# A decoder block's first phases: v kept unflipped, the long filter's matrices loaded row by row into the first phase and kept on the chip

## What is computed

```python
h = layernorm(x)                                      # 16 x 256 x 256
q, k, v = (silu(causal_dwconv(h @ W, w_conv)) for W, w_conv in ...)   # 4 taps per channel
beta, res = sigmoid(h @ Wb), sigmoid(h @ Wres + bres)
q, k = l2norm(q), l2norm(k)
inv = inverse of (I + strictly lower part of (beta k) k^T), in chunks of 32 tokens
long_fir[t, c]  = sum over j < 64 of fir_long[c, 63 - j] * v[t - j, c]    # one filter per channel
short_fir[t, c] = the same with 5 taps
```

## Time and profile before

| what | us |
|---|---|
| time, median of 3 runs | 1337.79 |
| lowest and highest of them | 1335.50, 1341.93 |
| profiled execution, from its first to its last instruction | 1347.3 |
| phase A in it | 0 to 245.2 |
| phase B in it | 245.4 to 324.2 |
| the rest in it | 324.5 to 1347.3 |
| DVE busy in phases A and B | 200.7 of 245 and 77.3 of 80 |

### The profile page before, as it was taken

The page is one execution under the profiler, slowest core; times in us unless marked ns, Lnnn a source line. Parts: engine busy times, 40 slices in busy tenths (PEclk is TensorE's granted clock), DMA queues, the critical chain, the costliest instruction groups (busy, mean ns, idle before and its releaser), DMA issues. The chain is left out here.

```text
span 1347.3 us, 28551 instructions
## 1 busy us (share of the span) xinstructions
PE 1128.1 (84%) x9177; PEld 829.4 (62%) x9251; DVE 957.8 (71%) x2132; ACT 900.2 (67%) x1743; POOL 658.3 (49%) x2200
## 2 busy tenths in 40 slices
PE   5989898783777879999999999999999887885756
PEld 4767676683566656766766776676676654443225
DVE  4999998698345666767777866876776666633985
ACT  4989998221343567778778878867877765453867
POOL 4777775663135455365465556446546544111007
PEclk9999999555567889899999989989989999997989
DMA  2444433894313333323434434334332342203106
GB/s 77 149 153 160 167 141 149 185 226 119 120 56 103 95 102 107 112 91 111 128 109 122 124 102 135 103 106 126 107 111 84 83 144 64 75 33 123 58 1 218
DMA packets 141779, 154.17 MB, mean 114 GB/s; under 512 B 48040, under 2 KB 106560, under 8 KB 141632
## 3 DMA queue, kind: packets, MB, share of 16 engines
q1 hardware_dynamic: 141632, 152.35, 37.5%
HBM read 93.32 MB, written 58.72 MB: 113 GB/s over the span
## 5 line engine op out<-in xcount | busy, mean ns | idle before, releaser
L2119 DVE TENSOR_REDUCE x_maxima<-x_psA 128x2 f32<-128x512 f32 x248 | 170.8, 689 | 116.3 <-PE x_psA L1447 114.4
L1703 ACT ACTIVATE x_PT<-x_psB 128x512 f32<-128x512 f32 x240 | 143.0, 596 | 53.8 <-PE x_psB L1471 49.5
L1710 ACT ACTIVATE x_psA<-x_mask_q 128x512 f32<-128x512 bf16 x239 | 142.5, 596 | 48.9 <-DVE x_maxima L2119 45.8
L297 DVE SCALAR_TENSOR_TENSOR a_conv<-a_ps_proj,taps,a_conv 128x253 f32<-128x253 f32 (+2 forms) x288 | 115.0, 470 | 10.6 <-ACT a_conv L364 10.6
L1447 PE MATMUL x_psA<-x_Ks,x_Qs 96*128 96x256 bf16 x496 | 99.1, 282 | 17.7 <-ACT x_psA L1710 17.2
L533 PE MATMUL a_ps_proj<-a_hT,wqkv 128*128 128x256 f32 x384 | 95.9, 401 | 6.4 <-DVE a_conv L297 3.8
L1471 PE MATMUL x_psB<-x_Qs,x_Ks 98*128 98x256 bf16 x480 | 93.2, 275 | 8.0 <-issue 6.4
L533 PEld LDWEIGHTS a_ps_proj<-a_hT,wqkv 128*128 128x128 f32 x384 | 73.1, 198 | 19.5 <-issue 6.1
L1863 POOL TENSOR_SCALAR x_parts_q<-x_rest 128x512 bf16<-128x512 f32 x16 | 23.9, 1496 | 115.1 <-DVE x_rest L2095 115.1
L1468 PE MATMUL x_psB<-x_mask_k,x_ident_bf 128*128 128x512 bf16 x170 | 66.2, 390 | 13.3 <-ACT x_PT L1703 10.8
L1485 PE MATMUL x_psO<-x_PT,x_V 128*32 128x256 f32 x1024 | 70.9, 396 | 1.1 <-ACT x_PT L1703 1.0
(11 more groups left out here) (390 smaller groups left out, 3344.6 us busy)
## 6 DMA issues: line engine op xcount, KB each, us to landing
scratch_keypack<-a_keypack SPq DMA_DIRECT2D x16, 768.0 KB, 3.3
c_keypack<-scratch_keypack SPq DMA_DIRECT2D x16, 768.0 KB, 4.7
x_Ks<-scratch_k_parts SPq DMA_DIRECT2D x192, 64.0 KB, 2.2
b_matrix<-in_long_padded SPq DMA_DIRECT2D x16, 512.0 KB, 6.9
scratch_k_parts<-x_parts_k SPq DMA_DIRECT2D x32, 192.0 KB, 2.4
scratch_q_parts<-x_parts_q SPq DMA_DIRECT2D x32, 192.0 KB, 2.3
x_Qs<-scratch_q_parts SPq DMA_DIRECT2D x32, 192.0 KB, 2.9
a_x_in<-in_x SPq DMA_DIRECT2D x16, 256.0 KB, 2.7
```

The lines of the kernel that those rows point to most:

```text
L297: nc.vector.scalar_tensor_tensor(acc, ps_proj[PROJ_BANK[p]][:, c, 0:L - j], taps[:, p, c, TAPS - 1 - j:TAPS - j], acc, ALU.mult, ALU.add). ...
L1703: nc.scalar.activation(PT[:, k % (2 * GROUP)], bank_B(b, k)[0], ACT.Exp, scale=XD ** -0.5).then_inc(pexp_ready, 1)
L1710: nc.scalar.activation(psA[:].rearrange("p t q -> p (t q)"), mask_q[:, k % 2].rearrange("p s k -> p (s k)"), ACT.Copy).then_inc(mask_writt ...
L2119: nc.vector.tensor_reduce(maxima[:, t, 2 * pair:2 * pair + 2], bank_A(b, k)[0], AX.X, ALU.max).then_inc(maxed, 1)
```

## The change

Phase A no longer flips v. ACT's `vtok` copies v straight into `v_windows[:, 1]`, and the store of v reads it there. Two DMAs of a new operation `win` copy v, shifted by 64 tokens, within SBUF into `v_windows[:, 0]`. `v_tok`, both flips, their matrices, their three copies and their waits are gone.

With v the right way up the band matrix has to be reversed instead, so each partition starts one element earlier than the one before it. The matrices of all 256 channels are kept in a new buffer `matrix` [128, 256, 64], and phase A loads it partition by partition: 8 rows in each of the turns 0 to 15, by four operations `rows0` to `rows3` of SP, two loads each. SP waits for all of them at the end of phase A.

Phase B has no matrix loads. One matmul per channel takes both windows (64 columns), and the two halves of the channels go to the two halves of the output's partitions. There are 16 groups of 8 channel pairs, with 8 buffers in PSUM. The result is stored by eight DMAs in two stages. The early loads for phase C are all issued at the start of phase B. To make room, the buffers of the inversion lie in `X32` and `shared` now, so that each of the transposes waits for the one before.

```diff
-A_ORDER = [(0, "ld_x"), (4, "silu_v"), (1, "rstd"), (5, "kpk"), (3, "proj_q"), (3, "tap_q"), (3, "conv_k"), (4, "tail"),
-           (4, "norms"), (4, "norm"), (2, "turn_h"), (2, "hTc"), (5, "flipA"), (4, "ktok"), (5, "st_p"), (4, "st_k"),
-           (3, "conv_q"), (5, "diag"), (4, "stap"), (5, "dk"), (5, "fA"), (3, "tanh"), (3, "silu_q"), (2, "proj_k"),
+A_ORDER = [(0, "ld_x"), (0, "rows0"), (4, "silu_v"), (1, "rstd"), (5, "kpk"), (3, "proj_q"), (3, "tap_q"), (3, "conv_k"), (4, "tail"),
+           (4, "norms"), (4, "norm"), (2, "turn_h"), (2, "hTc"), (4, "ktok"), (5, "st_p"), (4, "st_k"), (0, "rows1"),
+           (3, "conv_q"), (5, "diag"), (4, "stap"), (5, "dk"), (3, "tanh"), (3, "silu_q"), (2, "proj_k"),
            (4, "short1"), (3, "silu_k"), (3, "proj_v"), (3, "tap_v"), (4, "tok2"), (4, "vtok"), (2, "tap_k"), (2, "gate"),
-           (0, "stat"), (4, "short2"), (3, "st_hT"), (3, "gsc"), (4, "st_v"), (3, "tok0"), (3, "sq0"), (4, "short_t"),
-           (4, "stok"), (1, "xn"), (4, "flipB"), (2, "gbias"), (4, "ks"), (4, "ksT"), (3, "tok1"), (4, "fB"), (3, "sq1"),
+           (0, "stat"), (4, "short2"), (0, "rows2"), (3, "st_hT"), (3, "gsc"), (4, "st_v"), (4, "win"), (0, "rows3"), (3, "tok0"), (3, "sq0"), (4, "short_t"),
+           (4, "stok"), (1, "xn"), (2, "gbias"), (4, "ks"), (4, "ksT"), (3, "tok1"), (3, "sq1"),
            (4, "st_s"), (3, "conv_v")]
...
+W_LOADS = 16 * 9
+FIR_COLS = P + HB
+ROWS_PER_TURN = P // B
+P_PER_SEM = 16
...
-        v_tok = sb("a_v_tok", [P, TT, D])
...
-        short_tok = sb("a_short_tok", [P, TT, D])
+        short_tok = keep["shared"][:, 0, 2]
...
-        squares = sb("a_squares", [P, 2, TT, D])
+        squares = keep["shared"][:, 0, 0:2]
...
                 elif op == "st_v":
                     sp.wait_ge(v_tok_ready, b + 1)
-                    sp.dma_start(dram["v_tok"][b], v_tok[:]).then_inc(v_stored, 16)
+                    sp.dma_start(dram["v_tok"][b], keep["v_windows"][:, 1, :, b]).then_inc(v_stored, 16)
+                elif op[:4] == "rows":
+                    for i in range(ROWS_PER_TURN // 4):
+                        r = ROWS_PER_TURN * b + ROWS_PER_TURN // 4 * int(op[4]) + i
+                        taps_of = bass.AP(dram["long_padded"].tensor, P - 1 - r, [[0, 1], [FIR_COLS, D], [1, HB]])
+                        sp.dma_start(keep["matrix"][r:r + 1], taps_of).then_inc(taps_placed[r // P_PER_SEM], 16)
+                elif op == "win":
+                    sp.wait_ge(v_tok_ready, b + 1)
+                    sp.dma_start(keep["v_windows"][HB:P, 0, :, b], keep["v_windows"][0:HB, 1, :, b]).then_inc(window_set, 16)
+                    sp.dma_start(keep["v_windows"][0:HB, 0, 1, b], keep["v_windows"][HB:P, 1, 0, b]).then_inc(window_set, 16)
...
-            sp.dma_start(flip[:], dram["flip"]).then_inc(w_loaded, 16)
-            sp.dma_start(half_flip[:], dram["half_flip"]).then_inc(w_loaded, 16)
...
                 elif op == "vtok":
                     act.wait_ge(turned[2], b + 1)
-
-                    if b >= 1:
-                        act.wait_ge(v_stored, 16 * b)
-                        act.wait_ge(v_flipped, b)
-                        act.wait_ge(half_flipped, b)
-                    nc.scalar.activation(v_tok[:], ps_tok[2][:], ACT.Copy).then_inc(v_tok_ready, 1)
-                elif op == "fA":
-                    act.wait_ge(v_flipped, b + 1)
-                    nc.scalar.activation(keep["v_windows"][:, 1, :, b], ps_tok[2][:], ACT.Copy).then_inc(flip_kept, 1)
-                elif op == "fB":
-                    act.wait_ge(half_flipped, b + 1)
-                    act.wait_ge(window_zero, 1)
-                    nc.scalar.activation(keep["v_windows"][0:HB, 0, :, b], ps_tok[2][0:HB], ACT.Copy)
-                    nc.scalar.activation(keep["v_windows"][HB:P, 0, 1, b], ps_tok[2][HB:P, 1], ACT.Copy).then_inc(half_kept, 1)
+                    nc.scalar.activation(keep["v_windows"][:, 1, :, b], ps_tok[2][:], ACT.Copy).then_inc(v_tok_ready, 1)
...
                     else:
-                        after(b, (flip_kept, -1, 1), (half_kept, -1, 1), (v_tok_ready, -1, 1))
...
-                elif op == "flipA":
-                    pe.wait_ge(v_tok_ready, b + 1)
-                    after(b, (half_kept, 0, 1), (v_tok_ready, 0, 1), (flip_kept, -1, 1))
-                    nc.tensor.matmul(ps_tok[2][:].rearrange("p t c -> p (t c)"), flip[:], v_tok[:].rearrange("p t c -> p (t c)"),
-                                     start=True, stop=True).then_inc(v_flipped, 1)
-                elif op == "flipB":
-                    pe.wait_ge(v_tok_ready, b + 1)
-                    after(b, (v_tok_ready, 0, 1), (flip_kept, -1, 1), (half_kept, -1, 1))
-                    nc.tensor.matmul(ps_tok[2][0:HB].rearrange("p t c -> p (t c)"), half_flip[:, 0:HB],
-                                     v_tok[:].rearrange("p t c -> p (t c)"), start=True, stop=True)
-                    nc.tensor.matmul(ps_tok[2][HB:P, 1], half_flip[:, HB:P], v_tok[:, 0], start=True, stop=True).then_inc(half_flipped, 1)
...
-CG = 16
-GROUPS = D // CG
-DEPTH = 4
+CG = 8
+GROUPS = P // CG
+DEPTH = 8
 EARLY_AT = 4
-FIR_COLS = P + HB
 
 
 def phase_b(nc, sems, dram, keep, used, early):
...
-        matrix = [sb(f"matrix{i}", [P, CG, HB]) for i in range(DEPTH)]
-        M = sb("M", [P, NQ, CH, CH])
-        product = sb("product", [P, NQ, (CH // 2) * (CH // 2)])
-        lower = sb("lower", [P, CH, CH])
-        psum = [ctx.enter_context(nc.psum_tensor(f"b_ps{i}", [P, CG, TT, B], FP32)) for i in range(DEPTH)]
-        loaded = [sem(f"loaded{i}") for i in range(DEPTH)]
+        M_first = sb("M_first", [P, 1, CH, CH])
+        M_rest = keep["X32"][:, 0:(NQ - 1) * CH].rearrange("p (q i) j -> p q i j", q=NQ - 1)
+        product = keep["X32"][:, (NQ - 1) * CH:].rearrange("p (q s) c -> p q (s c)", q=NQ)
+        lower = keep["shared"][:, 1, 0:2].rearrange("p n t d -> p (n t d)").rearrange("p (i j) -> p i j", j=CH)
+        psum = [ctx.enter_context(nc.psum_tensor(f"b_ps{i}", [P, CG, 2 * TT * B], FP32)) for i in range(DEPTH)]
...
-                elif group == EARLY_AT + 2:
-                    sp.dma_start(early["keypack0"][:], dram["keypack"][0]).then_inc(early["pack_loaded"], 16)
-                elif group == EARLY_AT + 4:
-                    sp.dma_start(early["k_tok"][:, 0], dram["k_tok"][0]).then_inc(early["pack_loaded"], 16)
-                    sp.dma_start(early["hT0"][:], dram["hT"][0]).then_inc(early["hT_loaded"], 16)
-                elif group == EARLY_AT + 6:
-                    sp.dma_start(keep["shared"][:, 0, 0], dram["v_tok"][0]).then_inc(early["vs_loaded"], 16)
-                    sp.dma_start(keep["shared"][:, 0, 1], dram["short_tok"][0]).then_inc(early["vs_loaded"], 16)
...
-                pe.wait_ge(loaded[n], 16 * (group // DEPTH + 1))
...
-                for c in range(CG):
-
-                    for part in range(2):
-                        last = nc.tensor.matmul(psum[n][part * HB:part * HB + HB, c].rearrange("p t b -> p (t b)"),
-                                                matrix[n][:, c], keep["v_windows"][:, part, :, :, group * CG + c].rearrange("p t b -> p (t b)"),
+                for i in range(CG):
+                    for half in range(FC):
+                        c = half * P + group * CG + i
+                        last = nc.tensor.matmul(psum[n][half * HB:half * HB + HB, i], keep["matrix"][:, c],
+                                                keep["v_windows"][:, :, :, :, c].rearrange("p a t b -> p (a t b)"),
                                                 start=True, stop=True, skip_group_check=True)
                 last.then_inc(filtered, 1)
...
-            for q in (NQ - 1, 0, 1, 2):
-                nc.vector.transpose(M[:, q].rearrange("p i j -> p (i j)"), keep["diag"][:, q * CH:(q + 1) * CH].rearrange("p s c -> p c s")).then_inc(M_turned, 1)
+            for q in range(NQ):
+                if q > 0:
+                    dve.wait_ge(M_turned, q)
+                nc.vector.transpose(M_of(q, 1)[:, 0].rearrange("p i j -> p (i j)"), keep["X32"][:, q * CH:(q + 1) * CH].rearrange("p s c -> p c s")).then_inc(M_turned, 1)
...
-            nc.vector.memset(M[:].rearrange("p q i j -> p q (i j)")[:, :, 0:CH * CH:CH + 1], 1.0).then_inc(M_masked, 1)
-            dve.wait_ge(M_masked, 4)
-            for q in range(NQ):
+            for M in (M_first[:], M_rest):
+                nc.vector.memset(M.rearrange("p q i j -> p q (i j)")[:, :, 0:CH * CH:CH + 1], 1.0).then_inc(M_masked, 1)
+            dve.wait_ge(M_masked, 5)
+            for n, q in enumerate(reversed(range(NQ))):
                 at = slice(q * CH, (q + 1) * CH)
-                nc.vector.transpose(keep["X32"][:, at].rearrange("p s i -> p i s"), M[:, q])
+                if n > 0:
+                    dve.wait_ge(X_turned, n)
+                nc.vector.transpose(keep["X32"][:, at].rearrange("p s i -> p i s"), M_of(q, 1)[:, 0]).then_inc(X_turned, 1)
```

(30 more changed lines are left out.)

62 lines of the change are left out of this document (20 added, 42 removed).

## The result

The changed kernel takes 1500.6 us (median of 4 runs, 1493.22 to 1505.95) where the kernel before takes 1338.3 beside it: 1.120 times the time, with an interval of 1.116 to 1.125. That is 162 us more, where +208 was forecast. The profiled execution spans 1494.8 us.

The account below looks back on a forecast made before the run. No engine over 84% busy; A's turn near the DVE's work, B a DVE chain. Rows 328, other transfers 66, start 8 and last turns 50 end A at 452 us: +207 - 0.6 + 1.4 = +208, 1546 us; range 1410 to 1615.

Parts of the forecast that it names:

- The fullest microsecond of before: Phase A: each DMA engine moved 25.6 GB/s there, taken as the rate into one partition, so 2.56 us a row.
- the one-partition load of 8 KB: Phase C's load, the nearest row: 0.2 us at 39 GB/s, which makes 1.7 us a row load.
- the overlap: Phase A, turns 0 to 15: a fifth of 82 us of other transfers overlaps the row loads, leaving 66 us.
- The range's low end: Whole kernel: 1410 us, from 1.5 us a row with most of the rest overlapped.
- The drain: End of phase A: turns 16 to 20 after the last row lands, taken as 50 us.
- The turn: Phase A: 25 us of DMA a turn, keypack stores 25 us apart in turns 5 to 15; 13.35 us before.
- The chain of who waits for whom: Phase A: ACT's SiLU of q waits for a keypack store behind four row loads; x also stands behind up to four.
- The rival in which the loads are hidden: Phase A: rows take 0.28 us, below 0.9, and hide under the turn; 1335 us in all; chance 0.14.
- 1.7 and 4.4 us a row: Phase A rivals: as the 8 KB load went, 1436 us, chance 0.13; one piece at a time, 1781 us, chance 0.05.
- The flips' gain: Phase A: ACT work removed returns at most 11 us, about 6 expected, hidden under DMA except 0.6 at the end.
- +1.4: Phase B: six DVE waits of 0.18 us, a second memset and its wait lengthen the DVE chain by 1.4 us.
- The start: Phase A, in the hidden-loads rival: x of item 2 stands behind sixteen row issues of 0.57 us, +2 us.

Follow-up runs that it names:

- cols: Changed kernel with each of the 128 loads writing two channels into all 128 partitions, filters not reversed: 1351.1 us, ratio 1.0085 to the kernel before.
- order: Changed kernel with its rows reordered: eight successive rows lie four partitions apart each, then 64 away; 1412.8 us (one run).
- same_port: Changed kernel with eight successive rows in two groups of four partitions 32 apart, and B's PE filter waiting for the first transposes: 1525.3 us (one run).
- fill: Kernel late plus three matmuls of the flips' shapes in the flips' places, result unread, ACT's copies still away: 1336.6 us, ratio 0.999 to the kernel before.
- staged: Changed kernel with rows copied from HBM to an HBM scratch tensor, phase B loading and filtering as before the change: 1346.1 us, ratio 1.0057.
- late: Kernel staged with the row copies in turns 4 to 19 instead of 0 to 15: 1340.0 us, ratio 1.0032 to the kernel before.
- half: Changed kernel loading only half of the channels, 32 KB a row, used by phase B for both halves: 1366.9 us (one run).

## Why the forecast was right, and where its sum was off

**What decides.** Right, and shown: a row load of 65.5 KB into one partition takes 2.5 us when all sixteen engines do nothing else (forecast 2.56), and the same bytes over 128 partitions cost nothing of the kind (cols). The fullest microsecond of before, split by engine, gave this number; the one-partition load of 8 KB, 1.7 us, was the wrong neighbour, by the prediction's own reason that none of its pieces stands behind another. Where the limit sits was not quite right: the prediction put it on the single partition, and order and same_port show that the partitions of a group of four, and those 32 further, share it. In the changed kernel neighbours follow each other, so both give the same time. That one engine's rate before (25.6) and this shared limit (26) are the same number was read as cause; no run shows that it is more than luck. The Trainium skill (SBUF — State Buffer, "Door 1: The DMA port swizzle") has four neighbouring partitions behind one port at 27.6 GB/s, and partition p + 32 behind the same port as p, p + 64 behind another. The 26 GB/s, the 25 of same_port and the gain of order agree with it. The same page says under "Can I just issue two DMAs to hit both halves?" that two DMAs "serialize": it has 6% more for one tile at partition 0 and one at partition 64 than for a single one. Here successive one-partition loads to different ports moved 1.6 times as much (42 against 26 GB/s), so for loads that fill one port each the measurement decides otherwise.

**The term that was off: the overlap.** The sum let a fifth of the other 82 us of transfers run beside the rows, 66 us on top. (By its own terms the other transfers are 76 + 16 x 0.5 = 84 us, not 82; this changes little.) Measured: the rows begin at 8.5 us and need 128 x 2.52 = 323 us, and the twelfth keypack store, the head of turn 16, comes at 344.0. That leaves 344.0 - 8.5 - 323 = 13 us, so 69 of the 82 us were hidden. The last rows land a little after that store: they are issued up to 342 us, no row landed sooner than 6.3 us after its issue, and from 352 us on DMA is idle for 2 us. Counted to their landing it is 17 to 21 us, so **61 to 69 of the 82 us were hidden**. The stretches say as much: from 60 to 200 us the engines are no busier than with rows alone, and move 106 instead of 26 GB/s. My reading is that a transfer to other partitions or to HBM passes between the pieces that are held up; no trace shows single pieces. Hidden means here that they cost the queue little, not that they were quick: x of item 2, issued at 29.8 us behind sixteen rows, is there only at 58.0. And how much hides is no constant: in order the same working leaves 264.4 - 7.8 - 128 x 1.56 = 57 us, so either only some 25 us were hidden there, or the rows moved slower than 42 GB/s once other transfers ran. With 13 in place of 66 us the sum is 8 + 323 + 13 + 52 = 396 us, where A ended. This one term is 53 of the 57 us by which phase A came out under its forecast of +207; the difference of the medians, +162, stands 46 us under the +208.

**The range's low end** doesn't follow from its words. 1.5 us a row gives 1410 us with all of the 66 us on top; with most of the rest overlapped, 13 us on top, it gives 8 + 192 + 13 + 50 = 263 us for A and a time of 1357. The measured time lies inside either range.

**The drain** was right: 50 us forecast, 51.8 measured.

**The turn** was to be 25 us and was 21.3 (eight rows at 2.52 are 20.2). The 13.35 us that the prediction has for the turn of before is one pair of stores; from the first store to the twelfth it is 13.25. The chain of who waits for whom came out as written: ACT behind the keypack store, the DVE behind x, PE behind ACT. The rival in which the loads are hidden is refuted, as are 1.7 and 4.4 us a row for this order of rows.

**The flips' gain** was put at 6 us, hidden under DMA. It stayed hidden in the changed kernel, and no run shows it. The ACT waits of the DVE were read as ACT's time; fill takes 1.2 us a turn off ACT, its turns are no shorter (13.5 us against 13.25), and its time lies between 0.4% under that of before and 0.2% over it, so a gain of over 5 us is excluded there. What is more, without the flips' matmuls PE's granted clock drops from 1.00 to about 0.9 (cols, staged, late). The turns are then 0.15 us shorter in staged and half a us longer in cols and late; what of this is the clock's doing and what the loads' is not shown. Nor was there a run with the flips gone and no loads beside, so a small gain that the loads ate up stays possible. The prediction priced a clock of 1.2 GHz only under the 25 us of DMA.

**Phase B** was put at +1.4 and took +3.7. The waits between the transposes are in it about as forecast (the last four take 7.7 us against 7.1); what was missed is that the first four transposes themselves take 2.40 to 2.83 us instead of 1.90 while PE runs. In the kernel before, PE began 4 us later, when its first load had landed, and only the last of the four, from 250.9 us on, ran beside a PE that was busy throughout:

```profile
L728 DVE STREAM_TRANSPOSE b_M<-diag x4: 1861/1888/2148, 245.5 to 250.9; 128x1024 f32<-128x1024 f32 x4
```

Taking PE away gave 2.4 of the 3.7 us back (same_port, 80.1). The 16 loads and half of PE's work that leave phase B are worth nothing, as forecast: PE was busy 37.6 of 82.5 us, inside the 28 to 56 named.

**The start** was a term of the rival alone: rows ahead of item 2's x. In the changed kernel it is part of the DMA bound; elsewhere it costs 0.8 us at the first store in cols, 5.6 in staged and 17 in half, whose rows still go to single partitions; late takes it away.

## What to carry to other kernels

Before a load is moved under other work, count the partitions that it writes, not its bytes: 8 MB took 323 us partition by partition, and the kernel that loads them with as many DMAs over all partitions is 12 us slower than before, not 162. If loads must go to single partitions, let successive ones fall on different groups of four, and not 32 apart; this order alone saved 88 us here. And work that leaves an engine which is not the bound has to be tested against what it kept going: here the flips' matmuls kept PE's clock up, though what that was worth in time is at most a few us and not clear of noise.

## What the runs showed of the hardware that was not expected

- A share of 1.56 with 26 GB/s: DMA engines can all be busy and move a fourteenth of what they can (374 GB/s at a full share), and most of the other transfers' time still fits beside them (61 to 69 of 82 us; less in order).
- Three small matmuls in a turn of 13 us decide whether PE's granted clock is 1.00 or 0.89 over 140 us (fill against late), that is, whether it spends a fifth of the stretch at 1.2 instead of 2.4 GHz.
- A 128x1024 transpose on the DVE takes 1.90 us alone and 2.40 to 2.83 while PE is streaming weights and windows. The Trainium skill (SBUF — State Buffer, "SBUF: two separate sides") holds that only the port pair shared by DVE and GpSimd causes contention; GpSimd was busy 2.4 to 2.5 us in both stretches. The first transpose is the cleanest pair: while it runs, ACT and GpSimd are idle in both kernels, and it takes 2.43 us with PE busy and 1.90 with PE idle. These rows speak against the page. In the kernel before, a transpose beside a busy PE took 2.15 us, so by how much PE slows it depends on something that is open here. Through which resource PE slows the DVE no run here tells.
- Copies of 64 KB from HBM to HBM in 256-byte pieces landed in 2.6 us.
